# Local attention with undivided queries: each row's inverse query length becomes the scale of the exponential

## The reference, cut to what matters

```python
q = l2norm(q) * qs
k = l2norm(k) * ksc
q, k = rotary_xpos(q, k)      # q * cos * scale + rotate_half(q) * sin * scale, and so on
o = local_attention(q, k, v)  # sim = (8 q) . k, masked, softmax over the keys, times v
```

## Time and profile before

| | |
|---|---|
| median of 3 runs | 4838.58 us (4828.19 to 4843.67) |
| the profiled execution | 4835.97 us |
| its span, first to last instruction | 4833.9 us |
| PE busy | 3997.4 us (83%) |
| DVE busy | 3015.9 us (62%) |
| ACT busy | 2782.2 us (58%) |
| POOL busy | 2067.8 us (43%) |
| mean granted clock of PE | 0.927 of full speed |

### The profile page before, as it was taken

How to read it: one execution, slowest core, us unless ns; L and a number is a source line. 1 busy time by engine, 2 the same in 40 slices (tenths; PEclk the granted TensorE clock), 3 DMA queues, 4 the chain that set the end, 5 groups by cost and what they waited for, 6 DMA issues and landing times. The chain is left out here.

```text
span 4833.9 us, 54427 instructions
## 1 busy us (share of the span) xinstructions
PE 3997.4 (83%) x17076; PEld 2418.5 (50%) x17076; DVE 3015.9 (62%) x5743; ACT 2782.2 (58%) x6184; POOL 2067.8 (43%) x1350
## 2 busy tenths in 40 slices
PE   6787898788888888888987989888887888888846
PEld 4445554455545554455544555455544555445412
DVE  4426666667476674766657666666647667477464
ACT  3465557555575565665665655755557555665332
POOL 2204244544364451744426434444436445175334
PEclk9899999999999999999998999999999999999867
DMA  3020013111131111210121111311113111221212
GB/s 103 1 90 1 17 55 111 37 48 37 38 122 39 38 45 60 92 50 26 59 86 58 54 32 51 114 35 48 39 36 122 41 35 47 66 81 53 83 43 74
DMA packets 188824, 274.01 MB, mean 57 GB/s; under 512 B 23448, under 2 KB 102900, under 8 KB 188532
## 3 DMA queue, kind: packets, MB, share of 16 engines
q1 hardware_dynamic: 186340, 268.72, 17.5%
q10 hardware_dynamic: 2192, 1.70, 0.1%
HBM read 215.54 MB, written 54.79 MB: 56 GB/s over the span
## 5 line engine op out<-in xcount | busy, mean ns | idle before, releaser
L603 POOL TENSOR_TENSOR work<-work 128x512 f32<-128x512 f32 x512 | 665.5, 1301 | 1209.8 <-DVE work L663 1120.8
L1513 POOL TENSOR_TENSOR work<-work,minus_half 128x8 f32<-128x8 f32 x256 | 473.8, 1864 | 563.0 <-DVE work L1496 559.9
L1616 ACT ACTIVATE work<-psum,work 128x128 f32<-128x128 f32 (+1 forms) x1024 | 391.4, 396 | 403.2 <-DVE work L1638 402.8
L663 DVE SCALAR_TENSOR_TENSOR work<-work,psum 128x512 f32<-128x512 f32 x528 | 362.1, 686 | 412.0 <-ACT work L595 411.3
L571 PE MATMUL psum<-work,w_up 128*128 128x512 f32 x1024 | 544.1, 614 | 64.9 <-DVE work L663 61.3
L595 ACT ACTIVATE work<-psum 128x512 f32<-128x512 f32 x528 | 315.5, 598 | 433.9 <-PE psum L571 426.8
L577 PE MATMUL psum<-work,w_down 128*128 128x512 f32 x1024 | 539.0, 609 | 5.1 <-POOL work L603 5.1
L1441 PE MATMUL psum<-wqkv,xn 128*128 128x512 f32 x768 | 392.2, 638 | 56.8 <-PEq L386 40.2
L1581 PEld LDWEIGHTS psum<-work 128*128 128x128 f32 x3072 | 394.6, 200 | 61.7 <-issue 50.1
L1581 PE MATMUL psum<-work 128*128 128x64 f32 x3072 | 417.2, 281 | 9.3 <-ACT work L1603 8.6
L1570 PE MATMUL psum<-ident,work 128*128 128x128 f32 x1536 | 252.5, 290 | 152.7 <-ACT work L1616 124.7
(11 more groups left out here) (240 smaller groups left out, 8516.4 us busy)
## 6 DMA issues: line engine op xcount, KB each, us to landing
work<-expert_weight_rows SPq DMA_DIRECT2D x1024, 128.0 KB, 2.9
position_scores<-work SPq DMA_DIRECT2D x64, 768.0 KB, 3.5
work<-position_scores SPq DMA_DIRECT2D x64, 512.0 KB, 3.8
work<-state_readout_rows SPq DMA_DIRECT2D x72, 256.0 KB, 4.3
rows<-state_readout_rows SPq DMA_DIRECT2D x32, 256.0 KB, 4.0
sq<-state_readout_rows SPq DMA_DIRECT2D x24, 256.0 KB, 4.2
rows<-in_L_attn_q SPq DMA_DIRECT2D x8, 256.0 KB, 3.5
expert_weight_rows<-work SPq DMA_DIRECT2D x16, 128.0 KB, 2.3
```

The lines of the kernel that those rows point to most:

```text
L603: pool.tensor_tensor(h, h, self.weights[p % self.SLOTS], ALU.mult).then_inc(self.gated, 1)
L663: v.scalar_tensor_tensor(out=self.gate_h[p % 3][0:rows], in0=self.tanh_h[p % self.turns][0:rows], scalar=1.0, in1=bank(b, self.ups[p % sel ...
L1513: pool.tensor_tensor(half, half, b.minus_half[:].broadcast_to([128, LH]), ALU.pow).then_inc(self.inv_norm, 1)
L1616: ins = self.nc.scalar.activation(out[:, x, -n:] if t else out[:, x], self.scores(m)[:, x], ACT.Exp, bias=self.neg_max[i % 2][:, slot:slot ...
```

## The change

Queries are added up from their two rotary parts but no longer multiplied by their inverse lengths. POOL takes the power -1/2 of the keys' sums, adds the queries' parts (which now signals `q_rotated`), and then takes the power of the queries' sums into a small tile of its own (`inv_q`, 128x8 for a tile). The scores therefore are longer than they should be by each row's query length. The exponential takes that row's and head's inverse length as its scale, and the negated maximum, being its bias, is multiplied by the same number. `maxima` handles a pair of groups in one call: two reductions as before, a wait for them, a wait for the inverse lengths, and one product over both groups (128x8 or 128x4), which alone signals `maxed`. All exponentials of a pair wait for that signal. The mask's value is -1e30 in place of -3e38.

```diff
@@ project_vector
             if i >= 1:
-                dve.wait_ge(self.q_rotated, tile - 1)
+                dve.wait_ge(self.inv_lengths, tile - 1)
...
-            dve.wait_ge(self.inv_norm, 2 * tile + 1)
+            dve.wait_ge(self.inv_norm, tile + 1)
@@ project_gpsimd
+        power = b.minus_half[:].broadcast_to([128, LH])
         pool.wait_ge(self.clipped, tile + 1)
-        for half in (lens[:, LH:], lens[:, 0:LH]):
-            pool.tensor_tensor(half, half, b.minus_half[:].broadcast_to([128, LH]), ALU.pow).then_inc(self.inv_norm, 1)
+        pool.tensor_tensor(lens[:, LH:], lens[:, LH:], power, ALU.pow).then_inc(self.inv_norm, 1)
         pool.wait_ge(self.split, tile + 1)
-        pool.tensor_tensor(queries, queries, sine[:, 0:INNER], ALU.add).then_inc(self.added, 1)
-        pool.wait_ge(self.added, tile + 1)
-        pool.wait_ge(self.inv_norm, 2 * tile + 2)
-        queries = queries.rearrange("p (h d) -> p h d", d=LD)
-        pool.tensor_tensor(queries, queries, lens[:, 0:LH].unsqueeze(2).broadcast_to([128, LH, LD]), ALU.mult).then_inc(self.q_rotated, 1)
+        pool.tensor_tensor(queries, queries, sine[:, 0:INNER], ALU.add).then_inc(self.q_rotated, 1)
+        pool.tensor_tensor(self.inv_q[i % 2][:, t * LH:(t + 1) * LH], lens[:, 0:LH], power, ALU.pow).then_inc(self.inv_lengths, 1)
@@ exps
-        act.wait_ge(self.maxed, group + 1)
+        act.wait_ge(self.maxed, group // 2 + 1)
...
-                                            bias=self.neg_max[i % 2][:, slot:slot + 1], accum_out=self.sums[i % 2][:, at:at + 1])
+                                            scale=self.inv_q[i % 2][:, at:at + 1], bias=self.neg_max[i % 2][:, slot:slot + 1], accum_out=self.sums[i % 2][:, at:at + 1])
@@ maxima
-        t, heads, n = self.group(m)
-        at = 8 * t + self.slot(m)
-        dve.wait_ge(self.s_ready, self.GROUPS * i + m + 1)
-        self.nc.vector.tensor_reduce(self.neg_max[i % 2][:, at:at + len(heads)], self.scores(m), AX, ALU.max, negate=True).then_inc(self.maxed, 1)
+        v, half = self.nc.vector, self.GROUPS * i // 2 + m // 2
+        at, n = (8 if m else 0) + self.slot(m), len(self.group(m)[1])
+        for side in range(2):
+            dve.wait_ge(self.s_ready, self.GROUPS * i + m + side + 1)
+            ins = v.tensor_reduce(self.neg_max[i % 2][:, at + side * n:at + (side + 1) * n], self.scores(m + side), AX, ALU.max, negate=True)
+        ins.then_inc(self.peaked, 1)
+        dve.wait_ge(self.peaked, half + 1)
+        if i >= self.first:
+            dve.wait_ge(self.inv_lengths, 2 * (i - self.first) + (2 if m else 1))
+        maxima, lengths = (x[i % 2][:, at:at + 2 * n] for x in (self.neg_max, self.inv_q))
+        v.tensor_tensor(maxima.rearrange("p (s x) -> p s x", s=2), maxima.rearrange("p (s x) -> p s x", s=2),
+                        lengths.rearrange("p (x s) -> p s x", s=2), ALU.mult).then_inc(self.maxed, 1)
@@ attend_vector
             self.maxima(dve, i, 0)
-            self.maxima(dve, i, 1)
...
             if m in (1, 3):
                 self.maxima(dve, i, m + 1)
-                self.maxima(dve, i, m + 2)
@@ constants
-    mask = np.concatenate([np.where((d >= 0) & (d <= WINDOW), 0.0, NEG) for d in (near, wide)], axis=1).astype(f)
+    mask = np.concatenate([np.where((d >= 0) & (d <= WINDOW), 0.0, MASKED) for d in (near, wide)], axis=1).astype(f)
```

More of the change, by code:

```diff
@@ L35 @@
 NEG = -3.0e38
+MASKED = -1.0e30
 class Signal:
@@ L1390, in __init__ @@
         self.squared, self.summed, self.clipped, self.inv_norm = sem("qk_squared"), sem("squares_summed"), sem("sums_clipped"), sem("inverse_norms")
-        self.split, self.k_split, self.added, self.k_added, self.q_rotated, self.k_rotated = (
-            sem("query_parts_ready"), sem("key_parts_ready"), sem("query_parts_added"), sem("key_parts_added"), sem("queries_rotated"), sem("keys_rotated"))
+        self.inv_lengths, self.peaked = sem("inverse_query_lengths"), sem("scores_peaked")
+        self.split, self.k_split, self.k_added, self.q_rotated, self.k_rotated = (
+            sem("query_parts_ready"), sem("key_parts_ready"), sem("key_parts_added"), sem("queries_rotated"), sem("keys_rotated"))
         self.zeroed, self.s_ready, self.maxed, self.exped = sem("weights_zeroed"), sem("scores_ready"), sem("scores_maxed"), sem("scores_exped")
@@ L1411, in __init__ @@
         self.o_t = carve(4 * SEQ).rearrange("p (j n) -> p j n", j=4)
-        self.lens, self.neg_max, self.sums = two(16), two(16), two(16)
+        self.lens, self.neg_max, self.sums, self.inv_q = two(16), two(16), two(16), two(16)
     @staticmethod
```

## The result

The kernel after takes 4942.85 us (median of 4 runs, 4931.80 to 4951.97), the kernel before beside it 4841.12 us (4 runs). The ratio is 1.0214, 95% interval 1.0195 to 1.0234: slower by 102 us. The forecast was 4863 us, slower by 25, with a range up to 4914. The sign was right; the size was four times too small, and the time lies outside the range.

What follows compares the result with a forecast made beforehand. It took PE's time in local attention as set by the chain of scores, maximum, exponentials and transpose. Per turn 15.2 us added, 15.1 removed, 3 of new low clock: 3.1 longer, eight turns 25 us, so 4863 us (range 4797 to 4914).

Steps and rivals of the forecast that it cites:

- Pair, product, second pointer: Exponentials before PE's transposes: second reduction 0.60, product 0.20, scale from a tile 0.36, so 1.16 us added for m 0.
- the maxima that come earlier: Where DVE comes late to the maxima of m 2 or m 4, it comes earlier: 2.4 us a turn removed.
- The copies L1603: Slots with a projection, PE waiting for ACT's copy after m 1's exponentials: 0.36 us added three times, 1.0 us.
- The expert's wait: PE before L571, waiting for DVE's L663 behind the keys' products: 5.9 of 8.9 us a turn removed.
- Lone projection: Head of stage third: queries ready 3.1 us earlier, 1.6 us a turn removed, then bound by the keys.
- Product blocked behind POOL: Maxima's product behind a running POOL addition, m 4 in slots with a projection: 0.4 us added three times a turn.
- the rival: Maxima's product blocked 0.65 us at half of twelve waits: 4 us a turn on top, 4895 us; inside the forecast's 0.46.
- Clock given back: PE work behind shortened waits returns to full clock: 2, 1.5 and 1.2 us, 4.7 us a turn removed.
- New stretches: Low-clock work behind the longer m 0 waits: two or three a turn at 1 to 1.5 us, 3 us added.
- the chain alone decides: Rival: added 15.2 us stay, relief goes to L603 and table loads; turn 12 us longer, 4935 us; chance 0.11.

Runs made afterwards that it cites:

- the first part alone: Kernel before with POOL's part of the change alone: keys' power, sum, queries' power, no product, queries left undivided; 4744.06 us, ratio 0.9817.
- The third part alone: Kernel before with the maxima of a pair behind one signal and multiplied by ones from a tile; scale and POOL as before; 4987.02 us, ratio 1.0315.
- The same filler: Four small unused products on PE ahead of its wait for the transposes of m 0 and some m 4: kernel after 4877.30 us, kernel before 4825.23 us.

## Why the prediction was wrong in size

The forecast was +3.1 us a turn; measured is +15.1. The step that failed is the clock, put down as a gain where it was a loss: "4.7 given back" and "two or three in a turn at 1 to 1.5 us each are 3 us", together -1.7 us. In the profile after it is +4.8 (half of 60.9 - 51.3). That is 6.5 of the 12.0 us missed. 3.0 more are idle time, and 2.5 are busy time that the clock doesn't explain. Of the 4.8, 1.4 lie in L1058 (L1060 in the kernel after), in front of a wait that became 1.7 us a turn shorter, and cost no time. Counted by what lengthened the turn, the clock is 5.1 of the 12.0 and the waits are 4.4. With the medians, 102 us against 25, less was missed than in the profiled pair: 9.6 us a turn.

- *Pair, product, second pointer: 1.16 us for m 0.* Right where I read it: 1.29 became 2.45 us. The product took 168 ns where I took 200, the second pointer 88 to 93 where I took 90. PE's wait on the exponentials grew by 9.8 us a turn (15.0 to 24.8); the terms bearing on it, with the maxima that come earlier, add up to 12.1 + 0.9 + 1.2 - 2.4 - 0.5 = 11.3.
- *The copies L1603: 1.0 us.* Too small: 2.3 became 6.1 us a turn. I counted only the second pointer's time, 1.0. Alone, it brought 1.7 (the wait on this copy is 41.9 us over the span with the scale from a tile, and 28.0 before), and the pair with the product another 1.0 (36.2 us over the span), which I had taken as covered. POOL's part, which adds nothing to the chain, brought 0.9 (35.4 us over the span). The three make 3.6 of the 3.8. No term of mine allowed for the last, and why it lengthens this wait isn't shown.
- *The expert's wait: -5.9 us.* Measured 8.9 to 4.4, -4.4. Somewhat too large: L1502's excess is gone, L1481's is half gone.
- *Lone projection: -1.6 us.* POOL's wait is gone, but the wait on the keys took its place (L1448 <- L1506, 9.3 us over the span, became 23.5). The two together fell only from 12.6 to 9.9 us over the five turns, 0.5 us a turn. The prediction had said that the keys would then bind, and not what they would cost.
- *Product blocked behind POOL.* It occurs (up to 0.79 us, and 238 ns on average for four numbers, against 168 for eight). All that it adds over 168 ns is 1.1 us a turn, near the 1.2 that stand in the sum, and not the 4 of the rival.
- *Clock given back: -4.7 us.* Too large even in the first part alone: idle time fell by 11 us a turn, the stretch that I had read the earlier trace rows went to full clock, and busy time at 1.2 GHz in the whole turn didn't move (51.3 and 51.5), since other work, L1058 behind a wait of unchanged length above all, fell to the low level. Without L1058, 1.7 us came back. In the kernel after nothing is left of it. I summed places where clock comes back and none where it goes.
- *New stretches: 3 us.* Too small. I had written that waits for m 0 would become as long as those behind which the clock fell, and then priced a few of them. The third part alone costs 10.0 us a turn in this way (9.1 without L1058).
- *The 2.5 us left.* The up-projections L573 hold about 1.6 of them: their mean over the span went from 614 to 627 ns, more than the clock explains. Whether that is a short wait between two matmuls that the records count as busy stays open.

None of my tests for failure fired: the waits before L1570 grew by more than 8 us a turn, those before L571 shrank, and the granted clock moved from 0.927 to 0.925, by less than 0.005. The last was a poor test. The mean clock counts idle time as well, and the span grew. Twice (1 - 0.927) times 4833.9 us is 706 us at the low level, and twice (1 - 0.925) times 4950.2 is 743; a movement of 0.005 would be some 48 us at the low level.

Of the rivals, "the chain alone decides" at 4935 us is nearest to the time and still is not what happened: it took the relief as lost to L603, while most of the relief came, and it had the clock at 3 us. That its time is near is luck.

## What to carry to other kernels

In this kernel a wait on the engine that sets the time had two prices: its length, and the clock of the work behind it. The second can't be summed place by place from one profile: where many waits grow, take it as large as the waits themselves for the upper end of the range, and where they shrink, as nothing for the lower. Compare PE's busy time for the same number of matmuls, not the mean clock. Then look at what stands behind a slow stretch: in front of a wait on another engine it costs nothing. And try the order of a helper engine's instructions before its work is moved onto the chain: here one moved line gave 64 of the 86 us.

## What the runs showed of the hardware

- A wait of 1.29 us in slot 4 was followed by work at full clock, one of 2.45 us in the same place by 3.42 us for 1.98 us of work at a granted clock of 0.52. With four added matmuls (1.03 us together) in front, a wait of 1.59 us was again followed by full clock.
- A wait of the same 3.33 us before L1058 was followed by full clock in one kernel (2.20 us for six matmuls) and by the low level in another (4.21 us). The wait that followed on L1156 took up the difference: 3.63 and 1.48 us.
- The same filler lowered the busy time at the low clock in one kernel by more than a third (60.9 to 37.0 us a turn) and in another not at all (51.3 and 51.3), so its effect is read from a run, not assumed.
- In the kernel after, POOL's power over 128x8 took 2009 ns for the keys and 1867 for the queries, more than its addition over 128x512 (1325 ns).
